# A four-layer graph network: the edge loop of its third layer written out, with indices and features read in place

## The reference

```
def _L2_gnn_ref(x, edge_sh, edge_attr, edge_index, ...):
    pre = irrep_linear(x, W_pre0, b_pre0, W_pre1)
    p0, p1 = split_irreps(pre)
    ip1 = einsum('eum,eum->eu', p1[edge_dst], p1[edge_src]) / 3.0
    s0 = concatenate([p0[edge_dst], p0[edge_dst], ip1])
    ...                                   # gates, giving a new x
    w = ssp(edge_attr @ W_f1) @ W_f2 * (ssp(s0 @ W_s1) @ W_s2)
    w1, w2, w3, w4 = split(w, 4)
    x0e, x1e = split_irreps(x[edge_src])
    sh0, sh1 = edge_sh[:, 0], edge_sh[:, 1:4]
    out0 = w1 * x0e * sh0 + w4 * (einsum('eum,em->eu', x1e, sh1) / sqrt(3))
    out1 = w2 * x0e * sh1 + w3 * x1e * sh0
    out = segment_sum(merge_irreps(out0, out1), edge_dst)
```

## Time and profile before

| | us |
|---|---|
| median of 3 runs | 1738.77 |
| lowest and highest of them | 1738.32, 1747.2 |
| the profiled execution, whole | 1742.29 |
| its span on the core | 1740.3 |
| PE busy | 1550.7 (89%) |
| DVE busy | 1244.4 (72%) |
| POOL busy | 762.1 (44%) |
| ACT busy | 756.7 (43%) |

### The profile page before, as it was taken

How to read it: one execution, slowest core, us unless ns; L and a number is a source line. 1 busy time by engine, 2 the same in 40 slices (tenths; PEclk the granted TensorE clock), 3 DMA queues, 4 the chain that set the end, 5 groups by cost and what they waited for, 6 DMA issues and landing times. The chain is left out here.

```text
span 1740.3 us, 23387 instructions
## 1 busy us (share of the span) xinstructions
PE 1550.7 (89%) x5721; PEld 851.1 (49%) x5722; DVE 1244.4 (72%) x2250; ACT 756.7 (43%) x1764; POOL 762.1 (44%) x969
## 2 busy tenths in 40 slices
PE   5599999999977698985769999999999999995898
PEld 3255686444454698983523333333333333333343
DVE  8975798312249799893648998888899898987123
ACT  2254454000011788782135655555555555552010
POOL 0000797377306630000057777677676676750000
PEclk9799999999978698797869999899899899987899
DMA  8991000000010350001244443333333334420101
GB/s 215 51 181 45 1 2 1 7 16 16 7 43 0 110 77 1 1 1 31 85 130 122 121 121 112 105 120 120 99 119 121 101 116 121 120 64 1 55 6 42
DMA packets 96771, 122.03 MB, mean 70 GB/s; under 512 B 49835, under 2 KB 78145, under 8 KB 96705
## 3 DMA queue, kind: packets, MB, share of 16 engines
q1 hardware_dynamic: 80353, 49.65, 16.2%
q0 software_dynamic: 16352, 71.55, 13.2%
HBM read 100.80 MB, written 11.59 MB: 65 GB/s over the span
## 5 line engine op out<-in xcount | busy, mean ns | idle before, releaser
L1430 POOL DMA_INDIRECT far<-far_rows,far_index x150 | 173.3, 1155 | 121.2 <-POOL far_index L1426 112.4
L432 POOL TENSOR_SCALAR hot_i<-iota_row,il 128x128 f32<-128x128 bf16 x125 | 108.5, 885 | 179.6 <-DVE il L454 171.8
L1513 PE MATMUL f_ps<-w,soft 32*128 32x512 f32 x300 | 169.1, 643 | 9.6 <-ACT pair L1576 0.4
L613 POOL DMA_INDIRECT records<-recs,place_i x136 | 136.9, 1006 | 87.6 <-issue 40.8
L1461 POOL TENSOR_TENSOR pair<-far,pair 128x768 f32<-128x768 f32 x75 | 136.3, 1817 | 86.7 <-DVE pair L1637 86.7
L1530 PE MATMUL sum_ps<-pair,hot 128*128 128x512 f32 x300 | 159.7, 659 | 10.4 <-DVE hot L1613 10.0
L1480 PE MATMUL near_ps<-table,hot_t 128*128 x300 | 142.5, 606 | 15.9 <-DVE hot_t L1607 15.9
L1041 PE MATMUL sum_ps<-wx,prob_t 128*128 128x65 f32 x1024 | 138.8, 295 | 14.5 <-DVE prob_t L1073 14.5
L1517 PE MATMUL s_ps<-w,soft 32*128 32x512 f32 x300 | 148.4, 613 | 0.0
L1426 POOL COPY far_index<-far_node 128x1 int32 (+1 forms) x150 | 39.4, 263 | 247.3 <-DVEq L1600 247.3
L1041 PEld LDWEIGHTS sum_ps<-wx,prob_t 128*128 128x128 f32 x1024 | 136.5, 215 | 16.7 <-DVE prob_t L1073 16.7
(11 more groups left out here) (313 smaller groups left out, 3124.2 us busy)
## 6 DMA issues: line engine op xcount, KB each, us to landing
places<-local_rows SPq DMA_DIRECT2D x75, 128.0 KB, 3.2
pair<-zeros SPq DMA_DIRECT2D x1, 8576.0 KB, 59.3
s_all<-s_rows SPq DMA_DIRECT2D x8, 512.0 KB, 8.0
records<-empty_record SPq DMA_DIRECT2D x1, 2925.0 KB, 72.0
far<-far_rows,far_index POOLq DMA_INDIRECT x150, 4.3
recs<-in_edge_attr SPq DMA_DIRECT2D x1, 2176.0 KB, 26.9
records<-recs,place_i POOLq DMA_INDIRECT x136, 2.2
w_gcn<-in_L_gnn_W_gcn SPq DMA_DIRECT2D x2, 1024.0 KB, 8.2
```

The costliest lines, as they stand in the source:

```text
L432: nc.gpsimd.tensor_scalar(hot_i[:, g % 2, k, 1, :], c.iota_row[:], il[:, t + k:t + k + 1], None, ALU.is_equal).then_inc(hot_i_ready, 1)
L613: c.nc.gpsimd.indirect_dma_start(c.rows[:, :], bass.IndirectOffsetOnAxis(ap=c.place_i[:, t:t + 1], axis=0), c.recs[:, t, :], None).then_in ...
L1430: nc.gpsimd.indirect_dma_start(far[:, r, k, :], None, c.far[:, :], bass.IndirectOffsetOnAxis(ap=index[:, g:g + 1], axis=0)) \
L1513: nc.tensor.matmul(f_ps[:], soft[0:HID, b, k * P:k * P + P], c.w_2[0:HID, :], start=True, stop=True).then_inc(filt_f, 1)
```

## The change

The loop is gone: `staged` writes all 80 steps out for each engine, with numbers in place of registers. The two indirect DMAs of a superblock take their indices from `far_node` itself, so that two copies, two waits and two semaphore increments per superblock fall away on POOL. The copy of the features to `attr` falls away too, and PE transposes them from `recs`, where it need not wait for POOL's copy any more. The order of the stages, the rings and the other waits stay as they are. The core of the diff:

```
-def staged(engine, stages):
-    for u in range(HEAD):
-        for lag, stage in stages:
-            if u >= lag:
-                stage(u - lag, (u - lag) % UNROLL, (u - lag) // UNROLL)
-    with engine.Fori(0, (S - HEAD) // UNROLL) as i:
-        for k in range(UNROLL):
-            for lag, stage in stages:
-                ahead = HEAD + k - lag
-                stage(i * UNROLL + ahead, ahead % UNROLL, i + ahead // UNROLL)
-    for u in range(S, S + LAGS):
+def staged(stages):
+    for u in range(S + LAGS):
         for lag, stage in stages:
-            if u - lag < S:
+            if 0 <= u - lag < S:
                 stage(u - lag, (u - lag) % UNROLL, (u - lag) // UNROLL)
...
             def gather(u, r, turn):
...
-                    nc.gpsimd.tensor_copy(index[:, g:g + 1], far_node[:, bass.ds(u * TPS + k, 1)]) \
-                        .then_inc(index_copied, 1)
-                    pool.wait_ge(index_copied, u * TPS + (k + 1))
-                    pool.sem_inc(index_seen, 1)
+                    t = u * TPS + k
                     nc.gpsimd.indirect_dma_start(far[:, r, k, :], None, c.far[:, :],
-                                                 bass.IndirectOffsetOnAxis(ap=index[:, g:g + 1], axis=0)) \
+                                                 bass.IndirectOffsetOnAxis(ap=far_node[:, t:t + 1], axis=0)) \
                         .then_inc(arrived[g], 16)
...
             def take_fixed(u, r, turn):
                 pool.wait_ge(turned, free("turned", u, 2))
-                nc.gpsimd.tensor_copy(attr[:, r % 2, :, :], c.recs[:, bass.ds(u * TPS, TPS), 0:32]) \
-                    .then_inc(attr_ready, 1)
...
             def turn_inner(u, r, turn):
-                pe.wait_ge(attr_ready, u + 1)
...
-                    last = nc.tensor.transpose(turn_ps[0:HID, 1, k * P:k * P + P], attr[:, r % 2, k, :], c.ident[:])
+                    last = nc.tensor.transpose(turn_ps[0:HID, 1, k * P:k * P + P], c.recs[:, u * TPS + k, 0:32], c.ident[:])
...
-                    sh0 = c.recs[:, bass.ds(u * TPS + k, 1), R_SH]
+                    sh0 = c.recs[:, u * TPS + k, R_SH:R_SH + 1]
```

More of the change, by code:

```diff
@@ L1367, in interaction_edges @@
      weights_ready, dots_ready, thirds_ready, msgs_ready, sums_ready, sums_added) = (semaphore(c, "edge_" + n) for n in FIRST)
-    (hot_ready, soft_ready, soft_step, filt_f, step, index_copied, index_seen, index_made, sums_cleared, attr_ready,
+    (hot_ready, soft_ready, soft_step, filt_f, step, index_made, sums_cleared,
      q_ready, fourth_ready) = (
          semaphore(c, "edge_" + n) for n in (
-             "onehot_ready", "softplus_ready", "softplus_step", "attributes_filtered", "step", "index_copied",
-             "index_seen", "indices_made", "sums_cleared", "attributes_ready", "near_scalars_ready", "fourth_ready"))
+             "onehot_ready", "softplus_ready", "softplus_step", "attributes_filtered", "step", "indices_made", "sums_cleared", "near_scalars_ready", "fourth_ready"))
     arrived = c.gathered
@@ L1385, in interaction_edges @@
         hot = sb("hot", [P, 2, TPS, P])
-        attr = sb("attr", [P, 2, TPS, 32])
         attr_t = sb("attr_t", [HID, 2, SUP])
@@ L1408, in load_places @@
                 sp.wait_ge(hot_t_ready, free("onehots_turned", u, 3))
-                sp.dma_start(places[:, r % 3, :], c.local_rows[bass.ds(u * SUP, SUP)].partition_broadcast(P)) \
+                sp.dma_start(places[:, r % 3, :], c.local_rows[u * SUP:u * SUP + SUP].partition_broadcast(P)) \
                     .then_inc(places_arrived[r % 3], 16)
-            staged(sp, [(0, load_places)])
+            staged([(0, load_places)])
         @block.gpsimd
@@ L1465, in _ @@
             pool.wait_ge(index_made, 1)
-            staged(pool, [(0, gather), (1, take_fixed), (1, add_inner), (3, thirds)])
+            staged([(0, gather), (1, take_fixed), (1, add_inner), (3, thirds)])
         @block.tensor
@@ L1474, in gather_near @@
             def gather_near(u, r, turn):
[L1476 removed]
+                block_of = pe.value_load(c.block_reg[0:1, u:u + 1], min_val=0, max_val=NB - 1)
                 pe.wait_ge(hot_t_ready, made("onehots_turned", u))
@@ L1532, in add_up @@
                 last.then_inc(sums_ready, 1)
-            staged(pe, [(1, gather_near), (5, add_up), (2, turn_inner), (3, filters), (2, hidden)])
+            staged([(1, gather_near), (5, add_up), (2, turn_inner), (3, filters), (2, hidden)])
         @block.scalar
@@ L1641, in _ @@
             blocks = []
-            block_of = lambda u: dve.value_load(c.block_reg[0:1, bass.ds(u, 1)], min_val=0, max_val=NB - 1)
+            block_of = lambda u: dve.value_load(c.block_reg[0:1, u:u + 1], min_val=0, max_val=NB - 1)
             def messages(u, r, turn):
@@ L1679, in take_sums @@
                     .then_inc(sums_added, 1)
-            staged(dve, [(3, shift), (1, product), (0, one_hot_turned), (4, messages), (5, take_sums), (4, one_hot),
+            staged([(3, shift), (1, product), (0, one_hot_turned), (4, messages), (5, take_sums), (4, one_hot),
                          (3, weigh)])
```

13 lines of the change are left out of this document (5 added, 8 removed).

## The result

The changed kernel takes 1762.3 us (median of 4, 1757.2 to 1763.8), against 1740.1 for the kernel before beside it. The ratio is 1.0115, with a 95% interval of 1.0079 to 1.0151: slower by about 20 us, which is 1.2% and clear of the noise, and outside the range of the prediction. The profiled execution took 1763.5 us, 21.2 more than that of before.

The account below looks back on a forecast made before the run. DVE with POOL was to become the bound, at 9.0 us a step against PE's 8.25. Loop -0.4 us and filling -1.6 gave -2.0: median about 1736.8, said as 1736 us, range 1712 to 1754.

Parts of the forecast that it names:

- PE's step of 8.34 going to 8.25: PE: numeric addresses let ACT's copy out of f_ps start 0.09 us earlier; 5.9 us over 65 steps, if PE stays the bound.
- The features without a wait: PE: features come without a wait for POOL's copy; they were early before, so worth 0.
- POOL's gathers at 2 x 1.3 us: POOL: two back-to-back gathers take 2.6 us, 1.6 less than before; additions then start 5.9 us after `weigh` starts.
- DVE's chain, 3.1 + 4.8 from `weigh`, without the collision: DVE: L1648 starts about 3.1 us after `weigh` starts; from it to the next `weigh` takes 4.80 us undisturbed.
- The collision, 1.1 us: POOL's additions meet DVE's L1667 or L1659, costing 1.1 us, between 0.90 and 1.43; DVE's step becomes 9.0 us.
- The clock falls, 0.1 us a step: PE: 14 falls of its clock, each costing 0.5 us (bounds 0 and 2.35): 7 us, 0.1 per step.
- The filling, -1.6: Start of the pipeline: the shorter first pair of gathers gains 1.6 us, since all wait there for the first rows.
- Rival C: Instruction lists: the longer list stalls an engine 0.3 us in each of 66 steps; +20, 1757 us; chance 0.06.
- Rival A: POOL and DVE: additions miss, collision costs 0 to 0.6, PE is the bound again; about 1720 us; chance 0.29.
- 0.6 us later: POOL: if the gathers need 0.6 us more than 2.6, additions pass behind L1669 or meet `hot`; DVE's step 8.5.
- Rival B: DVE: additions block L1659 or L1667 and L1669 for all their 0.72 + 0.80 us; 1749 to 1758 us; chance 0.18.

Follow-up runs that it names:

- the wait: One added wait: POOL's additions to `inner` wait for DVE's `hot` of that step; 1715.0 us on the changed kernel, 1744.8 us on the kernel before.

## Why the prediction was wrong, point by point

The frame held. DVE with POOL became the bound, PE's 8.25 stayed in reach and was not used, and the collision of the additions with the last SBUF operations of `messages` decides the time. One term of the sum had the wrong size. For a profiled execution the forecast was -2.0 us, and +21.2 came. Of the 23.2 us between them the collision alone accounts for 65 x (1.46 - 1.1) = 23.4; the smaller misses below nearly cancel.

- **PE's step of 8.34 going to 8.25:** right. The looped kernels show 8.34, all written-out ones 8.25. The features without a wait were put at 0, and the experiment with them alone shows none.
- **POOL's gathers at 2 x 1.3 us:** nearly. They take 1.22 and 1.11 with 0.30 between, and from the end of `thirds` (1194.59) to the copy of `q` (1197.38) it is 2.8 us. The additions start at W + 6.06 in the median and not 5.9. The second gather starts 1.52 us after the first in most steps, over the 1.5 from which the prediction called this step wrong. It was, by 0.2 us in all, and that did not decide: the additions still start where the six L1638 end.
- **DVE's chain, 3.1 + 4.8 from `weigh`, without the collision:** right within 0.07. L1627 starts at W + 3.18, and without additions the shortest step is 8.03. What the prediction did not see is that `thirds` stretches the turned one-hots (0.92 for 0.34 at 1193.82), where I had let L1648 wait; the end is the same.
- **The collision, 1.1 us: the step that failed.** It measures 1.39 in 42 of the steps and about 1.62 in 17. The mean of 1.46 makes 3.17 + 4.80 + 1.46 = 9.43 of the 9.45 measured. I took a value between the rows of L1667 and L1659 because the copy to `attr` was gone. The experiment with the copy of the features kept, additions at W + 6.23, has 9.40: that copy had no part in it.
- **Why it was taken too low.** I held against a full loss that L1613 lost only 0.60 us beside additions of 0.72 + 0.80. The row says another thing. L1613 ran from 1033.39 to 1034.41, so it met the first addition (1033.40 to 1034.12) and lost 0.60 of its 0.72. The second, at 1034.19, stood beside L1637, which reads PSUM and lost nothing. The loss is nearly the whole of the addition, as long as the neighbour on DVE reads two SBUF tiles. That was in the rows.
- **The clock falls, 0.1 us a step:** too much. The steps with a fall are made good by PE in the next 8.25 ones, and DVE's two step lengths give 9.44 of the 9.45. PE waited for `hot` in 26 of the 65 steps, and not in each as the prediction had it. In the kernel before the 14 falls start 6.6 to 7.6 us into PE's step, 6 of them in the products of `filters`, where the prediction put them all, and 8 in those of `hidden`.
- **The filling, -1.6:** it gained 3.8, and not by the gathers. The second superblock's first product starts at 885.86, where it started at 884.93 before. The gain comes behind that, with the clock: from 889 to 913 us PE was granted 0.72 before and 0.99 after. The kernel with the indices in place has 0.72 in the same stretch of its filling (887 to 911), and superblock 9 starts 77.8 us after the first product, where it was 78.0 before. So the shorter gathers show 0.2 us there, and most of the 3.8 goes with a clock that stood otherwise in the two profiled executions, which the prediction did not foresee. The part after the last step gave 2.7 back; it lies between 190.3 and 194.8 us in all kernels here, and why it differs is not shown.

```profile
884.93 2.59 PE L1480 MATMUL near_ps<-table,hot_t 128*128 x4 [3.73 <-DVE hot_t L1607]
```

- **Rival C:** tested and out. **Rival A:** the price was well sized. With the additions past L1669, 0.5 us later, it is 1719.5 us, against the 1720 forecast for it. The "0.6 us later" at which it was to decide is borne out too.
- **Rival B** came true, and a little above its price: it had a step of 9.33 to 9.43, +19 us at most and 1758 at the top. The step is 9.45 and the median 1762.3.

The Trainium skill, "SBUF — State Buffer", section "SBUF: two separate sides", says that a VectorE operation with two SBUF inputs and a GpSimd operation which reads SBUF exclude each other for a whole instruction. For the additions the runs agree in size (0.93 us lost to one addition of 0.86, 1.39 to 1.62 to two of 1.44 to 1.87 together), and so do the PSUM readers, which lose nothing; that a loss can be above the addition's own length does not follow from it. By that rule the forecast would have been rival B. For POOL's copies with one input the measurement differs: 0.46 us lost beside 0.97.

## What to carry to other kernels

Price an operation that two engines may meet in by what reads SBUF on both sides, at its full length (here the copies with one input cost half of theirs), and look at which instruction stands beside it to the tenth of a microsecond: making POOL 1.5 us faster cost 24 us here, and moving the same additions by 0.5 us gave 43 back. An idle engine can be told when to work. A wait for a semaphore that costs the waiting engine nothing is a way to place its work beside the neighbour's PSUM operations.

When the step of a loop drops by relief on one engine, count the falls of PE's clock again before the gain is booked.

## What was not expected of the hardware

- **The number of clock falls differs between kernels with nearly the same work for PE.** In 65 steps of one profiled execution each, the kernel before and the changed one have 14. With the wait the looped kernel has 17 and the changed one 11, as without additions. The three written-out kernels with the index copies, at steps of 8.4 to 8.6 us, have 6 to 8. With the additions 0.5 us later, or with one addition, it is 10, and with the indices in place and the copy of the features kept, at 9.39 us, 16. The others have 11 to 13. So neither a longer step nor a DVE that paces means fewer falls by itself. Each fall costs 3.3 to 3.5 us where PE is the bound. Why 0.09 us of the step, or anything else, should make the difference was not tested and stays open.
- **One addition can cost more than its length** (0.93 for 0.86, or for 0.73 undisturbed) when it meets a row of short operations, and both can be stretched: additions of 0.72 take 0.87 and 1.00 beside L1638 and L1648.
- **A DVE operation with one tile and a column of scalars as inputs is held too**: the turned one-hots take 0.92 to 1.08 us for 0.34 beside `thirds`.
